# Macaron block on one core: routing steps and the attention's transposes placed one unit of experts later

## Chip, cores and metric

One core of one Trainium2 chip. The metric is the device time of one execution in microseconds, the median of the runs of a kernel. The kernel before ran three times: 587.32, 587.5 and 589.16 us, median 587.5.

## The reference

2048 tokens of width 128 pass three steps: half of a mixture-of-experts layer, an attention, half of the same mixture-of-experts layer again, each on a layer norm of its input and added to it.

```python
x = x + 0.5 * ffn(layernorm(x))
x = x + attn(layernorm(x))          # softmax over all 2048 tokens
x = x + 0.5 * ffn(layernorm(x))
# ffn: shared = silu(x @ Ws_up) @ Ws_down                     (64 hidden)
#      aff = x @ centroids.T ; the 8 of 64 experts with the largest aff + bias
#      w = sigmoid(aff) of those 8, divided by their sum, 0 for the other 56
#      result = shared + sum over experts of w_e * (silu(x @ W_up[e]) @ W_down[e])
```

## The kernel before

**Tiling.** The tokens are cut into 4 chunks of 512. The two mixture-of-experts layers make 8 chunks, n = 0 to 7 (chunk c of layer f is n = 4f + c); the attention lies between n = 3 and n = 4. All 64 experts are computed for all tokens, two experts at a time, so that hidden values fill 128 partitions. A chunk has 33 units: unit 0 is the shared expert (64 partitions), units 1 to 32 are pairs of experts. Each product of float32 quality is three matmuls of rounded parts (high times low, low times high, high times high).

**One unit u.** TensorE makes the hidden values in one of 4 PSUM buffers (`up`, L805 to L807). ScalarE applies silu in place (L380). VectorE multiplies by the experts' weights, spread over partitions in `wide` (`gate_unit`, L552). ScalarE copies the result as the high part (`hi_unit`, L391). The low part, the difference (`low_part`, L240), is made by GpSimd (POOL) in units where u % 3 is 1 or 2, and by VectorE in units where u % 3 is 0. TensorE multiplies by the down weights (`down`, L843 to L845) and accumulates over the 33 units. `down` runs 4 units behind `up`: in unit u TensorE does up(u), then down(u-4). up(u) reuses the hidden buffer of unit u-4, so it waits for gate(u-4) where GpSimd makes that unit's low part, and for the low part itself where VectorE does.

**Order of the work.** Each engine has its own loop over the units, written out by hand; `if u == ...` puts extra steps after the unit's own instructions. An engine does its instructions in this order and waits on semaphores at each. Within VectorE's unit u stand gate(u), then lo(u-1) if VectorE makes it, then the extra steps. ScalarE's unit has silu(u), hi(u-1), extra steps. GpSimd's unit has lo(u), if it is GpSimd's, and then its extra steps.

**Extra steps for the next chunk n+1** (`pro_...`, in chunks that have a next one in their layer: n = 0, 1, 2, 4, 5, 6): the layer norm's statistics (VectorE, u 0 and 2), rstd (GpSimd, u 3), normed values xn (VectorE, u 5 and 6, lines L575 to L579), their transposes `pro_xT` (TensorE, u 8, L856), split into high and low part (ScalarE u 9, VectorE u 9), affinities `pro_aff` (TensorE u 11, 12 matmuls; read by VectorE at u 12 and 13, L596 to L600), a reciprocal (`pro_top` 0, L607, u 14), top 8 (u 15, L611), and the mask of the chosen (u 17, L616, L618). `weights` (GpSimd, u 18, L332 and L333) waits for the mask; `pro_sum` (VectorE, u 20, L635 to L637) waits for `weights`; `normed_weights` (GpSimd, u 21, L338) waits for `pro_sum`; `pro_cw` (TensorE, u 24, L876) transposes; `pro_cwT` (ScalarE, u 25, L407) copies to `gates`. SyncE's queue (SP) stores them to DRAM and then loads them back, spread over 64 partitions each, one pair of loads a unit, up to 6 units ahead (`wide`, L299); its wait for `gates` stands before the loads of unit STORE = 30.

**Extra steps for the chunk before** (`epi_...`): the output is scaled (ScalarE u 5), transposed `epi_yT` (TensorE u 8, L849), added to x (VectorE u 9). In the first layer (n = 1, 2, 3) the attention's inputs follow: statistics (VectorE u 10), rstd (GpSimd u 14), normed xn2 (VectorE u 16 and 17), transposes `epi_xT` (TensorE u 20, L856), split `epi_hi` (ScalarE u 21) and `epi_lo` (VectorE u 21, L646), projections `epi_proj` (TensorE u 24, 28, 31).

**Counting.** `on_pool` decides who makes the low part; it makes some positions differ from their neighbours:

```python
def on_pool(u):
    return u % 3 != 0
```

Of the kernel before, what the change touches and what calls it, by code (L numbers as in the profile page):

```python
# [30 lines left out]
NH = 4  # L31
NB = 6
EARLY = 4
STORE = 30
GT = 2
PRE = 8
LEAD = 2
# [6 lines left out]
def macaron_kernel(nc, x_d, wup_d, wdn_d, wsup_d, wsdn_d, cent_d, bias_d, wq_d, wk_d, wv_d, gates_d, out_d):  # L44
# [21 lines left out]
    with ExitStack() as ctx:  # L66
# [146 lines left out]
        def on_pool(u):  # L213

            return u % 3 != 0
# [91 lines left out]
        @block.gpsimd  # L307
        def _(pool):
            steps = [0]

            def link(ins):

                steps[0] += 1
                ins.then_inc(s_pool, 1)
                pool.wait_ge(s_pool, steps[0])

            def rstd(k, n, stats, done):

                pool.wait_ge(stats, n + 1)
                ve, y = (rs[:, k, i, :] for i in range(2))  # L320
                link(nc.gpsimd.tensor_scalar(ve, mv[:, k, :, 1], EPS, None, ALU.add))
                nc.gpsimd.tensor_tensor(y, ve, mhalf[:, :], ALU.pow).then_inc(done, 1)

            def piece_lo(k):
                pool.wait_ge(s_whi, k + 1)
                nc.gpsimd.tensor_tensor(piece(k, 1), raw[:, k % NR, :], piece(k, 0).bitcast(F32), ALU.subtract).then_inc(s_w, 1)

            def weights(n):

                pool.wait_ge(p_sil, n + 1)  # L330
                pool.wait_ge(p_top, n + 1)
                link(nc.gpsimd.tensor_tensor(rec[:, :, :], rec[:, :, :], sil[:, :, :], ALU.mult))  # L332
                nc.gpsimd.tensor_tensor(rec[:, :, :], rec[:, :, :], rest[:, :, :], ALU.mult).then_inc(p_w, 1)  # L333

            def normed_weights(n):
                pool.wait_ge(p_inv, n + 1)
                inv = wsum[:, 1, :].unsqueeze(2).to_broadcast([P, TPC, E])
                nc.gpsimd.tensor_tensor(cw2[:, :, 0:E], rec[:, :, :], inv, ALU.mult).then_inc(p_cw, 1)  # L338

            link(nc.gpsimd.memset(ident[:, :], 0.0))  # L340
            nc.gpsimd.affine_select(out=ident[:, :], in_=ident[:, :], compare_op=ALU.not_equal, fill=1.0,
                                    base=0, pattern=[[-1, P]], channel_multiplier=1).then_inc(s_id, 1)
            link(nc.gpsimd.memset(mhalf[:, :], -0.5))
            for f in range(2):
                for c in range(NCH):
                    n = f * NCH + c
                    if c == 0:
                        rstd(0, n, p_st, p_rs)
                    if n == 0:
                        for k in range(PRE):  # L350
                            piece_lo(k)
                    for u in range(UNITS):
                        if on_pool(u):
                            low_part(nc.gpsimd, n * UNITS + u).then_inc(s_glop, 1)
                        if n == 0 and u % 2 == 0 and PRE + u // 2 < 2 * WP:
                            piece_lo(PRE + u // 2)
                        if c + 1 < NCH:
                            if u == 3:
                                rstd(0, n + 1, p_st, p_rs)
                            if u == 18:  # L360
                                weights(n + 1)
                            if u == 21:
                                normed_weights(n + 1)
                        if f == 0 and c and u == 14:
                            rstd(1, c - 1, e_st, e_rs)
                if f == 0:
                    rstd(1, NCH - 1, e_st, e_rs)

        @block.scalar
        def _(act):  # L370
# [66 lines left out]
            for f in range(2):  # L437
                for c in range(NCH):
                    n = f * NCH + c
                    if c == 0:  # L440
                        if f == 0:
                            piece_hi(0)
                            pro_hi(n)
                            for k in range(1, 6):
                                piece_hi(k)
                            pro_sil(n)
                            for k in range(6, PRE):
                                piece_hi(k)
                            for u in range(LEAD):
                                silu_unit(u, n)  # L450
                            pro_cwT(n)
                    for u in range(UNITS):
                        if c or u >= LEAD:
                            silu_unit(u, n)
                        if n == 0 and u % 2 == 0 and PRE + u // 2 < 2 * WP:
                            piece_hi(PRE + u // 2)
                        if u or c:
                            hi_unit(*((u - 1, n) if u else (UNITS - 1, n - 1)))
                        if c + 1 < NCH:
                            if u == 9:  # L460
                                pro_hi(n + 1)
                            if u == 15:
                                pro_sil(n + 1)
                            if u == 25:
                                pro_cwT(n + 1)
                        if c:
                            if u == 5:
                                epi_y(n - 1)
                            if f == 0 and u == 21:
                                epi_hi(c - 1)  # L470
                            if f == 0 and u in (25, 29, 32)[:1 if c == NCH - 1 else 3]:
                                epi_proj_hi(c - 1, (25, 29, 32).index(u))
                    if c == NCH - 1:
                        hi_unit(UNITS - 1, n)
                        if f == 0:
                            epi_proj_hi(c - 1, 1)
                        epi_y(n)
                        if f == 0:
                            epi_proj_hi(c - 1, 2)
                            epi_hi(c)  # L480
                            epi_proj_hi(c, 0)
                            epi_proj_hi(c, 1)
# [46 lines left out]
        def _(dve):  # L529
# [140 lines left out]
            for f in range(2):  # L670
                for c in range(NCH):
# [15 lines left out]
                    for u in range(UNITS):  # L687
# [3 lines left out]
                        if c + 1 < NCH:  # L691
                            if u == 0:
                                if f == 0:
                                    dve.wait_ge(s_x[c + 1], 16)
                                raw_stats(0, c + 1, (0, 1))
                            if u == 2:
                                stats(0, c + 1, p_st, (2, 3))
                            if u == 5:
                                normed(0, n + 1, c + 1, xn[f], p_rs, p_xn, (0, 1))
                            if u == 6:  # L700
                                normed(0, n + 1, c + 1, xn[f], p_rs, p_xn, (2, 3))
                            if u == 9:
                                pro_lo(n + 1)
                            if u == 12:
                                pro_aff(n + 1, 0)
                            if u == 13:
                                pro_aff(n + 1, 1)
                            if u == 14:
                                pro_top(n + 1, 0)
                            if u == 15:  # L710
                                pro_top(n + 1, 1)
                            if u == 17:
                                pro_top(n + 1, 2)
                            if u == 20:
                                pro_sum(n + 1)
                        if c:
                            if u == 9:
                                epi_x(n - 1, c - 1)
                            if f == 0:
# [3 lines left out]
                                    normed(1, c - 1, c - 1, xn2, e_rs, e_xn, (0, 1))  # L723
                                if u == 17:
                                    normed(1, c - 1, c - 1, xn2, e_rs, e_xn, (2, 3))
                                if u == 21:
                                    epi_lo(c - 1)
                                if u in (25, 29, 32)[:1 if c == NCH - 1 else 3]:
                                    epi_proj_lo(c - 1, (25, 29, 32).index(u))
# [72 lines left out]
        def _(pe):  # L802
# [107 lines left out]
            for f in range(2):  # L910
                for c in range(NCH):
# [10 lines left out]
                    for u in range(UNITS):  # L922
# [5 lines left out]
                        elif c:  # L928
                            down(UNITS - LAG + u, n - 1)
                        if c + 1 < NCH:  # L930
                            if u == 8:
                                pro_xT(n + 1)
                            if u == 11:
                                pro_aff(n + 1)
                            if u == 24:
                                pro_cw(n + 1)
                        if c:
                            if u == 8:
                                epi_yT(n - 1)
                            if f == 0:  # L940
                                if u == 20:
                                    epi_xT(c - 1)
                                if u in (24, 28, 31)[:1 if c == NCH - 1 else 3]:
                                    epi_proj(c - 1, (24, 28, 31).index(u))
# [117 lines left out]
```

## Time and profile before

| | us |
|---|---|
| median of 3 runs | 587.5 |
| the profiled execution, device time | 589.12 |
| its span, first to last instruction | 587.3 |
| TensorE matmul busy | 547.0 (93%) |
| VectorE busy | 440.8 (75%) |
| ScalarE busy | 408.0 (69%) |
| GpSimd busy | 274.8 (47%) |
| mean granted TensorE clock | 0.983 of full |

The profiled execution took 589.12 us on the device, 1.8 more than its span; that is 1.6 above the median, near the slowest of the three. Chunks begin at 14.20, 78.20, 134.72 and 190.17 us in the first layer, and at 381.72, 431.09, 481.25 and 531.39 in the second. Busy times of TensorE overlap, since matmuls are pipelined: it is better read by the starts of its instructions. "L805" is line 805 of the kernel. In a timeline, "x2" after a row means that two instructions in a row are merged, and the bracket tells how long the engine stood idle before and what released it.

### The profile page before, as it was taken

The numbers are of one execution on the slowest core, as the hardware profiler recorded it, in microseconds if no ns is written. First come the engines' busy times: TensorE is split into PE (matmuls) and PEld (weight loads), VectorE is DVE, ScalarE is ACT, GpSimd is POOL, SyncE is SP. The second block draws the span as 40 slices with busy tenths as digits, with TensorE's granted clock in tenths as the row PEclk, the third lists the DMA queues.
The fourth block names the chain that finished last, engine by engine and source line by source line (L and its number), as shares of the span: only waits on it lengthen the run. The fifth ranks groups of instructions, "written<-read, shape, count | busy, mean of one in ns | idle before, by whom it ended". The sixth has DMA issues, their size and how long they took to land.

```text
span 587.3 us, 8657 instructions
## 1 busy us (share of the span) xinstructions
PE 547.0 (93%) x2720; PEld 446.0 (76%) x2720; DVE 440.8 (75%) x913; ACT 408.0 (69%) x802; POOL 274.8 (47%) x241
## 2 busy tenths in 40 slices
PE   2489999899989999889999999899999999999996
PEld 2368777687768787668999989868777787877884
DVE  3787869967996587557677888888868958875663
ACT  3567776677767778356666665677776787687774
POOL 4478764656465666400000000045765666566563
PEclk9999999899999999969999999999999999999999
DMA  5465564355445555000000000036554465656552
GB/s 166 151 198 183 172 194 147 135 168 166 146 133 183 164 159 179 1 1 1 2 0 2 1 2 1 1 117 196 174 192 150 156 207 146 176 167 200 182 188 84
DMA packets 47837, 73.25 MB, mean 125 GB/s; under 512 B 8944, under 2 KB 13488, under 8 KB 47792
## 3 DMA queue, kind: packets, MB, share of 16 engines
q1 hardware_dynamic: 47792, 72.71, 39.5%
q8 instruction: 21, 0.34, 0.2%
q14 instruction: 24, 0.20, 0.1%
HBM read 70.58 MB, written 2.10 MB: 124 GB/s over the span
## 4 chain that ended last, share of the span: by engine, by line
PE 76%; DVE 13%; issue 3%; ACT 3%; DMA 2%; POOL 2%; SPq 1%; POOLq 0%; DVEq 0%; ACTq 0%
PE lrow L805 12%; PE lrow L807 11%; PE lrow L806 11%; PE bank L843 8%; PE bank L844 8%; PE bank L845 8%; PE bank L849 6%; PE bank L986 3%; PE bank L988 3%; PE bank L987 3%; DVE gated L552 2%; DVE rs L577 2%; DVE rs L575 1%; PE bank L807 1%; PE bank L806 1%
## 5 line engine op out<-in xcount | busy, mean ns | idle before, releaser
L240 POOL TENSOR_TENSOR gpart_lo<-gated,gpart_hi 128x512 fp32r<-128x512 f32 x176 | 226.6, 1294 | 197.8 <-ACT gpart_hi L391 194.2
L380 ACT ACTIVATE lrow<-lrow 128x512 f32<-128x512 f32 (+1 forms) x256 | 149.7, 585 | 63.5 <-PE lrow L807 62.0
L552 DVE TENSOR_TENSOR gated<-lrow,wide 128x512 f32<-128x512 f32 x170 | 116.5, 685 | 50.2 <-ACT lrow L380 46.4
L391 ACT CAST gpart_hi<-gated 128x512 fp32r<-128x512 f32 x176 | 107.9, 613 | 8.3 <-DVE gated L552 7.7
L843 PE MATMUL bank<-gpart_lo,wdn_hi 128*128 128x512 f32 x256 | 102.2, 399 | 1.1 <-POOL gpart_lo L240 1.0
L844 PE MATMUL bank<-gpart_hi,wdn_lo 128*128 128x512 f32 x256 | 101.3, 396 | 0.0
L845 PE MATMUL bank<-gpart_hi,wdn_hi 128*128 128x512 f32 x256 | 101.1, 395 | 0.0
L552 DVE TENSOR_TENSOR lrow<-lrow,wide 128x512 f32<-128x512 f32 x78 | 54.0, 693 | 28.7 <-ACT lrow L380 28.7
L391 ACT CAST gpart_hi<-lrow 128x512 fp32r<-128x512 f32 (+1 forms) x88 | 52.0, 591 | 30.4 <-DVE lrow L552 30.2
L751 DVE TENSOR_TENSOR pT_lo<-bank,pT_hi 128x512 fp32r<-128x512 f32 x64 | 43.7, 684 | 24.5 <-ACT pT_hi L496 23.7
L240 DVE TENSOR_TENSOR gpart_lo<-lrow,gpart_hi 128x512 fp32r<-128x512 f32 (+1 forms) x88 | 59.9, 681 | 1.3 <-ACT gpart_hi L391 0.6
L843 PEld LDWEIGHTS bank<-gpart_lo,wdn_hi 128*128 128x128 f32 x256 | 48.4, 189 | 14.0 <-POOL gpart_lo L240 3.1
L845 PEld LDWEIGHTS bank<-gpart_hi,wdn_hi 128*128 128x128 f32 x256 | 48.5, 190 | 11.4
L844 PEld LDWEIGHTS bank<-gpart_hi,wdn_lo 128*128 128x128 f32 x256 | 48.5, 190 | 10.9
L489 ACT ACTIVATE prow<-lrow,nmax 128x512 f32<-128x512 f32 x64 | 44.3, 694 | 14.8 <-DVE nmax L664 14.8
L496 ACT CAST pT_hi<-bank 128x512 fp32r<-128x512 f32 x64 | 37.9, 592 | 23.8 <-PE bank L849 23.6
L805 PE MATMUL lrow<-xnT_lo_a,wup_hi 128*128 128x512 f32 x128 | 53.5, 418 | 0.5 <-DVE gpart_lo L240 0.5
L805 PE MATMUL lrow<-xnT_lo_b,wup_hi 128*128 128x512 f32 x128 | 52.5, 410 | 0.0
L807 PE MATMUL lrow<-xnT_hi_a,wup_hi 128*128 128x512 f32 x128 | 51.7, 404 | 0.0
L806 PE MATMUL lrow<-xnT_hi_a,wup_lo 128*128 128x512 f32 x128 | 51.7, 404 | 0.0
L807 PE MATMUL lrow<-xnT_hi_b,wup_hi 128*128 128x512 f32 x128 | 50.5, 395 | 0.0
L806 PE MATMUL lrow<-xnT_hi_b,wup_lo 128*128 128x512 f32 x128 | 50.1, 391 | 0.0
(171 smaller groups left out, 997.6 us busy)
## 6 DMA issues: line engine op xcount, KB each, us to landing
wide<-gates_dram SPq DMA_DIRECT2D x496, 128.0 KB, 3.0
raw<-in_w_up SPq DMA_DIRECT2D x8, 256.0 KB, 3.6
raw<-in_w_down SPq DMA_DIRECT2D x8, 256.0 KB, 3.9
x<-in_x SPq DMA_DIRECT2D x4, 256.0 KB, 4.0
gates_dram<-gates SPq DMA_DIRECT2D x8, 128.0 KB, 2.2
out_dram<-x SPq DMA_DIRECT2D x4, 256.0 KB, 3.2
raws<-in_wq SPq DMA_DIRECT2D x1, 64.0 KB, 2.1
raws<-in_wk SPq DMA_DIRECT2D x1, 64.0 KB, 2.1
```

What stands on the lines that cost most here:

```text
L240: return eng.tensor_tensor(gpart[1][0:m, U % NGP, :], gated_at(U)[0:m, :], gpart[0][0:m, U % NGP, :].bitcast(F32), ALU.subtract)
L380: nc.scalar.activation(dst[0:m, :], hid[U % NH][0:m, :], ACT.Silu).then_inc(s_silu, 1)
L391: nc.scalar.copy(gpart[0][0:m, U % NGP, :], gated_at(U)[0:m, :]).then_inc(s_ghi, 1)
L489: nc.scalar.activation(prow[:, j * CH:(j + 1) * CH], lrow[:, j * CH:(j + 1) * CH], ACT.Exp, bias=nmax[:, t % 2:t % 2 + 1], accum_out=psums ...
L552: nc.vector.tensor_tensor(gated_at(U), a, b, ALU.mult).then_inc(s_gated, 1)
L751: nc.vector.tensor_tensor(pT[1][at], tb[q % 2][:, :].rearrange("p (k n) -> p k n", n=P), pT[0][at].bitcast(F32), ALU.subtract).then_inc(a_ ...
L805: nc.tensor.matmul(out, a[0], b[1], start=True, stop=False)
L806: nc.tensor.matmul(out, a[1], b[0], start=False, stop=False)
L807: return nc.tensor.matmul(out, a[0], b[0], start=False, stop=True)
L843: nc.tensor.matmul(y, w[0], g[1], start=(u == 0), stop=False)
L844: nc.tensor.matmul(y, w[1], g[0], start=False, stop=False)
L845: nc.tensor.matmul(y, w[0], g[0], start=False, stop=(u == UNITS - 1)).then_inc(s_down, 1)
```

## The change

Steps are placed one unit later on every engine: on GpSimd `weights` (18 to 19) and `normed_weights` (21 to 22); on ScalarE `pro_hi`, `pro_sil`, `pro_cwT` and `epi_hi`; on VectorE `pro_lo`, both steps of `pro_aff`, the three of `pro_top`, `pro_sum` and `epi_lo`; on TensorE `pro_xT`, `pro_aff`, `pro_cw` and `epi_xT`; on SyncE's queue the store of the gates (30 to 31). The norms (VectorE u 5, 6, 16, 17), `epi_yT`, `epi_x`, rstd and the projections stay.

```diff
-STORE = 30
+STORE = 31
 # GpSimd
-                            if u == 18:
+                            if u == 19:
                                 weights(n + 1)
-                            if u == 21:
+                            if u == 22:
                                 normed_weights(n + 1)
 # ScalarE
-                            if u == 9:
+                            if u == 10:
                                 pro_hi(n + 1)
-                            if u == 15:
+                            if u == 16:
                                 pro_sil(n + 1)
-                            if u == 25:
+                            if u == 26:
                                 pro_cwT(n + 1)
-                            if f == 0 and u == 21:
+                            if f == 0 and u == 22:
                                 epi_hi(c - 1)
 # VectorE
-                            if u == 9:
+                            if u == 10:
                                 pro_lo(n + 1)
-                            if u == 12:
+                            if u == 13:
                                 pro_aff(n + 1, 0)
-                            if u == 13:
+                            if u == 14:
                                 pro_aff(n + 1, 1)
-                            if u == 14:
+                            if u == 15:
                                 pro_top(n + 1, 0)
-                            if u == 15:
+                            if u == 16:
                                 pro_top(n + 1, 1)
-                            if u == 17:
+                            if u == 18:
                                 pro_top(n + 1, 2)
-                            if u == 20:
+                            if u == 21:
                                 pro_sum(n + 1)
-                                if u == 21:
+                                if u == 22:
                                     epi_lo(c - 1)
 # TensorE
-                            if u == 8:
+                            if u == 9:
                                 pro_xT(n + 1)
-                            if u == 11:
+                            if u == 12:
                                 pro_aff(n + 1)
-                            if u == 24:
+                            if u == 25:
                                 pro_cw(n + 1)
-                                if u == 20:
+                                if u == 21:
                                     epi_xT(c - 1)
```

## Rows read from the trace of the kernel before

**Rows 1.** The page: the chain that ended last, by engine.
```profile
PE 76%; DVE 13%; issue 3%; ACT 3%; DMA 2%; POOL 2%; SPq 1%; POOLq 0%; DVEq 0%; ACTq 0%
```
**Rows 2.** Timeline of TensorE, chunk 5, pro_xT and up(10): start us, us, instruction, [idle].
```profile
444.92 0.59 PE L856 MATMUL bank<-ident,xn_b 128*128 128x128 f32 x2 [0.49 <-DVE xn_b L579]
...
447.17 0.40 PE L805 MATMUL lrow<-xnT_lo_b,wup_hi 128*128 128x512 f32 x1
```
**Rows 3.** Timeline of VectorE: xn (2,3) and lo(6) of chunk 5; lo(6) of chunk 4.
```profile
444.53 0.59 DVE L579 TENSOR_SCALAR xn_b<-x,mv,rs 128x128 f32<-128x128 f32 x2
...
445.64 0.68 DVE L240 TENSOR_TENSOR gpart_lo<-lrow,gpart_hi 128x512 fp32r<-128x512 f32 x1
...
395.91 0.68 DVE L240 TENSOR_TENSOR gpart_lo<-lrow,gpart_hi 128x512 fp32r<-128x512 f32 x1
```
**Rows 4.** Timeline of TensorE: chunk 4's up(10); chunk 1's epi_xT (unit 20), up(26).
```profile
397.01 0.40 PE L805 MATMUL lrow<-xnT_lo_b,wup_hi 128*128 128x512 f32 x1
...
112.61 0.33 PE L856 MATMUL bank<-ident,xn 128*128 128x128 f32 x1 [1.57 <-DVE xn L579]
...
123.06 0.39 PE L805 MATMUL lrow<-xnT_lo_a,wup_hi 128*128 128x512 f32 x1
```
**Rows 5.** Windows after that wait, chunks 1 and 2: us, busy, PEclk, DMA share, GB/s.
```profile
113.38:116.80 3.42, 3.42 (x10) 2.65 (x11) 3.32 (x6) 2.91 (x6) 1.83 (x2) 0.53 0.27 93
...
169.90:173.26 3.36, 3.14 (x13) 2.27 (x14) 3.26 (x6) 2.86 (x6) 1.77 (x2) 1.00 0.26 93
```
**Rows 6.** Timeline of VectorE, chunk 5: gate(12), aff, gates 13, 16, mask, 19, lo(18), sum, 22.
```profile
452.81 0.70 DVE L552 TENSOR_TENSOR lrow<-lrow,wide 128x512 f32<-128x512 f32 x1 [1.44 <-ACT lrow L380]
453.42 0.41 DVE L596 TENSOR_SCALAR rec<-bank 128x256 f32<-128x256 f32 x1
...
454.21 0.69 DVE L552 TENSOR_TENSOR gated<-lrow,wide 128x512 f32<-128x512 f32 x1
...
459.10 0.67 DVE L552 TENSOR_TENSOR gated<-lrow,wide 128x512 f32<-128x512 f32 x1
...
461.77 1.55 DVE L618 TENSOR_TENSOR rest<-rest,biased_b 128x256 f32<-128x256 f32 x1
...
463.85 0.67 DVE L552 TENSOR_TENSOR gated<-lrow,wide 128x512 f32<-128x512 f32 x1
464.59 0.69 DVE L240 TENSOR_TENSOR gpart_lo<-lrow,gpart_hi 128x512 fp32r<-128x512 f32 x1
...
466.24 0.73 DVE L636 TENSOR_SCALAR wsum<-wsum 128x4 f32<-128x4 f32 x1
...
467.69 0.68 DVE L552 TENSOR_TENSOR gated<-lrow,wide 128x512 f32<-128x512 f32 x1
```
**Rows 7.** Timeline of GpSimd, chunk 5: lo(16) and lo(17), weights, lo(19) and lo(20), normed weights.
```profile
460.50 2.54 POOL L240 TENSOR_TENSOR gpart_lo<-gated,gpart_hi 128x512 fp32r<-128x512 f32 x2 [1.63 <-ACT gpart_hi L391]
463.47 0.75 POOL L332 TENSOR_TENSOR rec<-rec,sil 128x256 f32<-128x256 f32 x1 [0.42 <-DVE rest L618]
464.30 0.74 POOL L333 TENSOR_TENSOR rec<-rec,rest 128x256 f32<-128x256 f32 x1
465.65 2.54 POOL L240 TENSOR_TENSOR gpart_lo<-gated,gpart_hi 128x512 fp32r<-128x512 f32 x2 [0.61 <-ACT gpart_hi L391]
468.15 0.61 POOL L338 TENSOR_TENSOR cw<-rec,wsum 128x256 f32<-128x256 f32 x1
```
**Rows 8.** Instructions of line L618, minimum, median and maximum in ns.
```profile
L618 DVE TENSOR_TENSOR rest<-rest,biased_b x4: 425/1556/1557, 376.1 to 511.9; 128x256 f32<-128x256 f32 x4
```
**Rows 9.** Timeline of TensorE, chunk 5: up(22) and up(26).
```profile
465.34 0.50 PE L805 MATMUL lrow<-xnT_lo_b,wup_hi 128*128 128x512 f32 x1
...
471.47 0.40 PE L805 MATMUL lrow<-xnT_lo_b,wup_hi 128*128 128x512 f32 x1
```
**Rows 10.** Timeline of TensorE, chunk 3: down(17) in unit 21.
```profile
221.29 0.50 PE L843 MATMUL bank<-gpart_lo,wdn_hi 128*128 128x512 f32 x1
```
**Rows 11.** Timeline of SyncE's queue, chunk 5: the store of the gates.
```profile
472.55 0.48 SPq L280 DMA_DIRECT2D gates_dram<-gates  x1
```

## The prediction

> **What bounds the kernel now.** First the chain that ended last: TensorE holds 76% of it, VectorE 13% and GpSimd 2% [rows 1]. So TensorE's stream of matmuls sets the time, and the other engines count only where TensorE waits for them. Next, therefore, the starts of `up` in TensorE's timeline, unit by unit. From up(22) to up(26) of chunk 5 pass 6.13 us [rows 9]; less some 0.55 for `pro_cw` and two restarts, that is 1.40 us a unit, six matmuls at full rate. A unit that takes longer has an extra step or a wait. The waits that stand out are two. In each of the six chunks with a next one, `pro_xT` waits in unit 8 for the last normed tiles: 0.49 us on the matmul row, 0.8 in the stream with the restart [rows 2, 3]. And in chunks 1 and 2 `epi_xT` waits in unit 20 for xn2, 1.57 us and a bit more [rows 4]. After that wait the granted clock was 0.53 for 3.4 us in chunk 1 (near the lower of the two levels, 1.2 GHz) and 1.00 in chunk 2 after the same wait [rows 5]: the penalty is not regular.
>
> Then VectorE's timeline between units 12 and 24, which shows how little slack lies behind TensorE. In chunk 5 gate(12) comes after 1.44 us idle, and from there the engine works without a pause until lo(18) at 464.59, and up(22), which needs lo(18), starts at 465.34, 0.75 later, at once [rows 6, 9]. GpSimd has room there: after lo(17) it stands idle and takes `weights` (0.83 + 0.74 = 1.57 us) ahead of lo(19) [rows 7].
>
> **What is moved, and what it saves.** Nothing is added or removed; every instruction stays on its engine, so only waits can change.
>
> *`pro_xT`, unit 8 to 9.* Its last tile xn starts at 444.53 [rows 3], and TensorE now comes to it a unit (1.40) later, so this wait goes. What is late next is lo(6), which frees the buffer of up(10): it starts at 445.64 [rows 3], +0.75 gives 446.39, against up(10) at 447.17 before [rows 2]. Saved: 0.78. Chunk 6 repeats chunk 5, and chunks 1 and 2 show the same pattern. In chunk 4 lo(6) at 395.91 gives 396.66 against 397.01 [rows 3, 4]: 0.35 saved. In chunk 0, where unit 8's wait is longer but lo(6) is as late, I take 0.35 too.
>
> *`pro_hi`, `pro_lo`, `pro_aff` on TensorE* move together with it, in units where nobody waited: 0. Their cover is VectorE's idle 1.44 before gate(12) [rows 6]; TensorE's 12 short matmuls now stand ahead of up(13), and that idle time moves to before gate(13).
>
> *The first half of the routing, on VectorE.* Before, the first affinity step (0.79, from 453.42 to 454.21) ran between gate(12) and gate(13) [rows 6]. Now it follows gate(13). In chunk 5, with the 0.78 gained, gate(13) comes at 453.43. From gate(13) to the mask L618 it was 7.56; to that come 0.79 and one gate, 0.60, since gate(18) is now ahead of it: L618 at 462.4. Such a gate is followed on GpSimd by its low part 1.40 later (459.10 to 460.50), which takes 1.27 [rows 6, 7]; so lo(17) runs from 461.7 to 462.9.
>
> What L618 costs there: it took 0.43 us at its shortest and 1.56 at its median [rows 8]; in chunk 5 it ended at 463.32, just behind GpSimd's lo(17) (460.50 + 2.54 = 463.04) [rows 6, 7]. So I read its length as a wait for that operation and let it end at 463.2, 0.3 after lo(17), and not 1.55 after its start. The Trainium skill, page "SBUF — State Buffer", section "SBUF: two separate sides", states that VectorE and GpSimd share a port pair as an exclusive lock, held for the whole instruction by whichever starts first; by that L618 ends with lo(17), as I take it, while with a fixed 1.55 up(22) would wait 0.7 longer, and the sum below would be about 4 us more. The trace agrees with the lock (0.43 alone against 1.56).
>
> Then gate(19) 463.15, lo(18) 463.75, up(22) at 464.5, where TensorE wants it (465.34 - 0.78 = 464.56). No wait, the gain is still there.
>
> *The second half: `weights`, `pro_sum`, `normed_weights`.* Here the positions matter. Units 18 and 21 are multiples of 3, in which GpSimd has no low part; 19 and 22 are not. `weights` now stands behind lo(19), and `normed_weights` behind lo(22). Chunk 5: lo(19) 464.55 to 465.82; `weights` to 467.39 (+1.57). VectorE, through with gate(21) at about 465.6, stands in `pro_sum` waiting for it, with gate(22) and lo(21) queued behind: 1.8 us. GpSimd then runs lo(20) until 468.66; TensorE wants it for down(20) at 464.56 + 2 x 1.40 + 0.70 = 468.05 and waits 0.6. The second step of `pro_sum`, 0.73 long before and then ending with lo(19) (466.97 against 466.92) [rows 6, 7], now ends with lo(20), at 468.7. gate(22) 468.8 (467.69 before), lo(21) 469.4, so up(25) at 470.15, where TensorE would have been at 469.4 even after the first wait: 0.7 more. lo(22) 470.2 to 471.47, `normed_weights` (0.61) to 472.1; TensorE reaches `pro_cw` at 470.15 + 1.40 = 471.55 and waits 0.55. With the transposes (0.36) and restart, up(26) is at 472.55 against 471.47 [rows 9]. **Net in chunk 5: +1.1 us**, although 0.8 had been gained.
>
> *Copies and stores behind it.* `pro_cwT` then ends near 475 and the store goes out some 2.5 us after 472.55 [rows 11]. What queues behind it on SP are the loads for units 31 and 32 and of the next chunk, 6 units (8 us) ahead of use: 0, as the landing takes 3 us. Were that cover gone, each late load would cost its lateness once.
>
> *`epi_xT`, unit 20 to 21, `epi_hi`, `epi_lo` (chunks 1 and 2).* The mask now stands behind the norms, so xn2 is ready near 110.3 and the transposes' wait of 1.57 goes. But gate(17) stands behind the norm's first half at 109.2, lo(17) runs to 111.85, and down(17), wanted at 110.6, waits 1.3; lo(18) makes up(22) wait 0.4 (113.4); then as above `weights` ends at 116.3, lo(20) at 117.55 (wait 0.65), and `epi_lo`, last in VectorE's unit 22 (118.9), releases the first projection at 119.6 (wait 1.3). Then there is no wait at `pro_cw`, and up(26) is at 122.2 against 123.06 [rows 4]: -0.9. Chunk 2, 1.1 us shorter before because the clock stayed up, ends the same: +0.2. Chunk 3 has no next chunk; there down(17) waited for lo(17) until 221.29 [rows 10], after the transposes, which had run within that wait; now they come after it: +0.35.
>
> **The sum.** Chunk 0 +1.5, 1 -0.9, 2 +0.2, 3 +0.35, 4 +1.5 (chunk 5's 1.1 + 0.78 - 0.35), 5 and 6 +1.1 each, 7 and attention 0: **+4.85 us**. Against the profiled execution: span 587.3 to 592.1, device time 589.12 to 594.0. Its own time is 1.6 above the median 587.5, so the median should go to 592.3 us. Bounds for what no row shows, the phase between VectorE and GpSimd in the new order: at best the second-half chain costs half (0.9 a chunk instead of 1.85 in chunks 0, 4, 5, 6, 0.5 less in 1 and 2), sum about 0; at worst VectorE's tiny steps each meet a GpSimd operation and lose up to 0.7 more a chunk, sum near 9.
>
> **The rivals.** A measurement of this kernel tells 0.3%, 1.8 us, from no change.
>
> *A, the forecast*: up to half the gains kept, the GpSimd chain costs more. Chance 0.59, 589.5 to 595.5.
>
> *B, the same with the clock falling.* Three waits within 4 us come where two did. A stretch at 0.53 for 3.42 us [rows 5] loses 1.6 us. For it: chunk 1. Against: chunk 2, same wait, no fall. In three chunks it would be +4.8, some 597. Chance 0.14.
>
> *C, faster.* The waits at xn and xn2 go and nothing takes their place: 4 x 0.78 + 2 x 0.35, and what unit 20's wait cost with the slow stretch, 4.0 in chunk 1 and 3.0 in chunk 2; 10.8 in all, 576.7 us. It is decided at `pro_sum`: if `weights` is done when VectorE gets there (I have it 1.8 us late), nothing queues. For it: VectorE's queue may be later than I have it, so that it covers the wait. Against: the four units of lead are TensorE's only slack and rows 6 and 9 show it used up. Chance 0.14; most of it lies at 580 to 585.
>
> *D, no difference.* Gains and chain cancel, the bound at best above: 587.5. Chance 0.13.
>
> Faster by over 0.3% 0.14, within 0.3% 0.13, slower 0.73. The range 587 to 597 leaves out C and the tail of B.
>
> **What would show it.** Right: units 8 lose their wait; VectorE stands idle ahead of `pro_sum`'s reduce (L635) for over 1 us, released by GpSimd's L333; TensorE waits in units 24 and 25, for low parts of GpSimd and VectorE and for `cw`; `epi_proj` waits for x2T_lo; `weights` comes after lo(19). Wrong: L635 without idle time before it, or up(26) no later than before in chunks 5 and 6; or a wait of the loads (`wide`), which I put at 0.

## The result, and the profile after

The changed kernel took 593.59 us (median of 4 runs, 593.07 to 594.83) against 587.6 (4 runs, 587.32 to 589.16): ratio 1.0092, 95% interval 1.0073 to 1.0112. It is slower by 0.9% (the two medians alone give 1.0102, inside the interval); the forecast was 592.3 in a range of 587 to 597. The profiled execution took 593.69 us, its span 591.9.

The page of the changed kernel, the lines that answer to the table of before and to [rows 1]:

```profile
span 591.9 us, 8657 instructions
PE 546.1 (92%) x2720; PEld 440.9 (74%) x2720; DVE 434.8 (73%) x913; ACT 408.8 (69%) x802; POOL 274.2 (46%) x241
PE 65%; DVE 15%; POOL 8%; issue 4%; ACT 4%; DMA 2%; SPq 1%; POOLq 0%; DVEq 0%; ACTq 0%
```

The same instructions, the same count; VectorE is even 6 us less busy, 4.5 of them in the mask L618, which waits less (8 times, 10.0 us in all before and 5.5 after). But the chain that ended last has 8% on GpSimd where it had 2%, and 65% on TensorE where it had 76%. Its waits say where, with the total in us, the number of times and the longest:

```profile
PEld bank L843 <- POOL gpart_lo L240: 11.7, 13, 1.5
DVE wsum L635 <- POOL rec L333: 10.2, 6, 1.7
PEld lrow L805 <- DVE gpart_lo L240: 6.8, 13, 1.1
PEld bank L876 <- POOL cw L338: 3.0, 4, 0.8
```

Before, the first line read 3.1 us in 5 times, the third 2.4 in 5, and the second had no entry at all.

GpSimd in chunk 5, which starts at 433.20 here and at 431.09 before; compare [rows 7]:

```profile
463.89 1.29 POOL L240 TENSOR_TENSOR gpart_lo<-gated,gpart_hi 128x512 fp32r<-128x512 f32 x1 [0.40 <-ACT gpart_hi L391]
466.80 1.30 POOL L240 TENSOR_TENSOR gpart_lo<-gated,gpart_hi 128x512 fp32r<-128x512 f32 x1 [1.62 <-ACT gpart_hi L391]
468.06 0.73 POOL L332 TENSOR_TENSOR rec<-rec,sil 128x256 f32<-128x256 f32 x1
468.87 0.73 POOL L333 TENSOR_TENSOR rec<-rec,rest 128x256 f32<-128x256 f32 x1
469.56 1.28 POOL L240 TENSOR_TENSOR gpart_lo<-gated,gpart_hi 128x512 fp32r<-128x512 f32 x1
472.43 1.30 POOL L240 TENSOR_TENSOR gpart_lo<-gated,gpart_hi 128x512 fp32r<-128x512 f32 x1 [1.59 <-ACT gpart_hi L391]
473.68 0.62 POOL L338 TENSOR_TENSOR cw<-rec,wsum 128x256 f32<-128x256 f32 x1
```

The order is lo(17), lo(19), `weights`, lo(20), lo(22), `normed_weights`. The engine stands idle 1.62 us before lo(19) although the mask has been ready since 465.5, and does `weights` only afterwards.

VectorE in the same stretch (compare [rows 6]), from the mask on:

```profile
464.57 0.90 DVE L618 TENSOR_TENSOR rest<-rest,biased_b 128x256 f32<-128x256 f32 x1
465.39 0.68 DVE L552 TENSOR_TENSOR gated<-lrow,wide 128x512 f32<-128x512 f32 x1
465.99 0.67 DVE L240 TENSOR_TENSOR gpart_lo<-lrow,gpart_hi 128x512 fp32r<-128x512 f32 x1
...
469.64 0.42 DVE L635 TENSOR_REDUCE wsum<-rec 128x4 f32<-128x256 f32 x1 [1.70 <-POOL rec L333]
470.09 0.78 DVE L636 TENSOR_SCALAR wsum<-wsum 128x4 f32<-128x4 f32 x1
...
471.01 0.69 DVE L552 TENSOR_TENSOR gated<-lrow,wide 128x512 f32<-128x512 f32 x1
471.62 0.68 DVE L240 TENSOR_TENSOR gpart_lo<-lrow,gpart_hi 128x512 fp32r<-128x512 f32 x1
```

L635 comes after 1.70 us of waiting for L333, with gate(22) (471.01) and lo(21) (471.62) behind it. And TensorE (compare [rows 2, 9]):

```profile
448.51 0.50 PE L805 MATMUL lrow<-xnT_lo_b,wup_hi 128*128 128x512 f32 x1
...
466.72 0.50 PE L805 MATMUL lrow<-xnT_lo_b,wup_hi 128*128 128x512 f32 x1
...
470.90 0.50 PE L843 MATMUL bank<-gpart_lo,wdn_hi 128*128 128x512 f32 x1 [0.42 <-POOL gpart_lo L240]
...
472.35 0.50 PE L805 MATMUL lrow<-xnT_lo_b,wup_hi 128*128 128x512 f32 x1 [0.50 <-DVE gpart_lo L240]
...
474.35 0.63 PE L876 MATMUL bank<-ident,cw 128*64 128x128 f32 x4 [0.34 <-POOL cw L338]
474.74 0.47 PE L805 MATMUL lrow<-xnT_lo_b,wup_hi 128*128 128x512 f32 x1
```

Counted from the chunk's start, up(10) is at 15.31 us (16.08 before: 0.77 gained), up(22) at 33.52 (34.25 before: still gained), and then come three waits, at down(20), up(25) and `pro_cw`. up(26) is at 41.54 against 40.38: 1.16 lost.

The same reading for each chunk, in us against the trace of before (chunk 5's and 6's lengths: 51.40 and 51.36 against 50.15; chunk 3 is read at its last `up`; the attention is the stretch from there to the first `up` of chunk 4):

| | chunk 0 | 1 | 2 | 3 | attention | 4 | 5 | 6 | sum |
|---|---|---|---|---|---|---|---|---|---|
| forecast | +1.5 | -0.9 | +0.2 | +0.35 | 0 | +1.5 | +1.1 | +1.1 | +4.85 |
| measured | +1.52 | -0.61 | +0.47 | +0.46 | -1.31 | +1.64 | +1.24 | +1.22 | +4.63 |

Not all of these figures repeat from trace to trace, which the experiments below need. In a second trace of the kernel before, chunk 0 was 0.50 shorter and chunk 1 was 1.05 shorter (its slow stretch of [rows 5] was absent); chunks 2 to 6 were as long to 0.04. So every figure for chunk 1 that is taken against the first trace, here and below, makes the other version look 1.05 better than it is, where its own trace has no such stretch: against the second trace the changed kernel's chunk 1 stands at +0.44, like chunk 2. The attention, too, has one length in some traces and another in others (last experiment).

### The profile page after: what moved, and what is told of

It is laid out like the page before. It is cut to its first block, busy times and chain, and to the rows that moved or that the text cites. A ratio compares the mean times of both kernels' runs of the same rounds, so it can differ in the third digit from the quotient of the medians.

```text
span 591.9 us, 8657 instructions
## 1 busy us (share of the span) xinstructions
PE 546.1 (92%) x2720; PEld 440.9 (74%) x2720; DVE 434.8 (73%) x913; ACT 408.8 (69%) x802; POOL 274.2 (46%) x241
## 4 chain that ended last, share of the span: by engine, by line
PE 65%; DVE 15%; POOL 8%; issue 4%; ACT 4%; DMA 2%; SPq 1%; POOLq 0%; DVEq 0%; ACTq 0%
PE lrow L805 10%; PE lrow L807 9%; PE lrow L806 9%; PE bank L843 7%; PE bank L845 6%; PE bank L844 6%; PE bank L849 5%; POOL gpart_lo L240 5%; DVE gated L552 3%; PE bank L986 3%; PE bank L988 3%; PE bank L987 3%; DVE gpart_lo L240 2%; ACT gpart_hi L391 2%; DVE rec L607 1%
```

## The experiments

Ratios are to the kernel before on the same chip; there its median was 589.3 to 589.4 us, so that ratios, not times, are to be compared over the groups.

**GpSimd's two steps put back in the changed kernel.**

```diff
-                            if u == 19:
+                            if u == 18:
                                 weights(n + 1)
-                            if u == 22:
+                            if u == 21:
                                 normed_weights(n + 1)
```

> The changed kernel with GpSimd's two steps alone put back: weights in unit 18, normed_weights in unit 21; everything else stays one unit later. Theory (the loss comes from weights standing behind lo(19), so that pro_sum on VectorE waits 1.7 us for it, and from normed_weights standing behind lo(22)): the idle time of VectorE before L635 falls from 10.2 us to under 1, TensorE's waits in units 24 and 25 of chunks 0, 4, 5, 6 vanish, while the gain of the later pro_xT stays. up(26) against the kernel before: -0.3 in chunks 0 and 4, -0.75 in 5 and 6, -2.4 and -1.4 in 1 and 2, +0.5 in 3: about 582 us, faster than both kernels. Rival (VectorE's own later order, lo(21) and epi_lo behind more work, makes TensorE late): the waits in units 24 and 25 stay, 592 us or more.

Measured: 581.29 us, ratio 0.9865 (0.984 to 0.9891). Two places of an `if` turn a loss of 0.9% into a gain of 1.35%. GpSimd and VectorE in chunk 5, where lo(17) is at 454.97:

```profile
454.97 1.30 POOL L240 TENSOR_TENSOR gpart_lo<-gated,gpart_hi 128x512 fp32r<-128x512 f32 x1 [0.39 <-ACT gpart_hi L391]
456.69 0.74 POOL L332 TENSOR_TENSOR rec<-rec,sil 128x256 f32<-128x256 f32 x1 [0.42 <-DVE rest L618]
457.51 0.74 POOL L333 TENSOR_TENSOR rec<-rec,rest 128x256 f32<-128x256 f32 x1
458.20 2.56 POOL L240 TENSOR_TENSOR gpart_lo<-gated,gpart_hi 128x512 fp32r<-128x512 f32 x2
...
458.93 0.41 DVE L635 TENSOR_REDUCE wsum<-rec 128x4 f32<-128x256 f32 x1
```

`weights` runs in what was GpSimd's idle time before lo(19), and L635 has no wait, in any of the six chunks. Read at up(28), behind all extra steps of the next chunk, the chunks stand against the trace of before at -1.32, -2.72, -1.64, +0.44, -0.43, -0.76 and -0.77 (0 to 6): 5 and 6 as expected, 4 better by 0.1, 1 and 2 by 0.3 and 0.2. The gain as a whole is larger than expected: some 8 us against the 589.34 of this chip, where about 582 against 587.5 had been 5.5. In the trace, 1.0 of the difference is chunk 0 and 1.2 the attention, neither of which repeats. Chunk 0's figure differs by 1.5 us between two versions whose order of steps in it is the same (+1.52 in the changed kernel, +0.05 with the attention's steps put back), so it can carry no argument.

**The same two steps moved alone, in the kernel before** (18 to 19, 21 to 22).

> The kernel before with GpSimd's two steps alone moved: weights to unit 19, normed_weights to unit 22. Theory: pro_sum, here still in VectorE's unit 20, stands some 2.7 us waiting for weights behind lo(19), and normed_weights comes behind lo(22), which needs gate(22), which is behind pro_sum; pro_cw, still in TensorE's unit 24, waits about 4 us for it. Some 4 us in each of six chunks: about 612 us, far slower than the change as a whole. Rival (where GpSimd's two steps stand does not matter, since GpSimd is idle half of the time): 587.5 us.

Measured: 625.14 us, ratio 1.061 (1.0594 to 1.0625): +36 us, the theory's sign and mechanism, and nearly half as much again as it said. The waits of that kernel:

```profile
PEld bank L876 <- POOL cw L338: 23.6, 6, 4.1
DVE wsum L635 <- POOL rec L333: 15.7, 6, 2.6
```

2.6 us at L635 and 4 at `pro_cw`, as reckoned. What was missing is for the most part the clock: chunks 1 and 2 lost 4.9 and 6.0, the others 6.0 to 7.4. After such a wait the granted clock falls, as these windows of its chunk 4 show (the stretch with the wait, the 4.8 us from `pro_cw` on, and the next 9 us; us, busy time of PE, PEld, DVE, ACT and POOL, then PEclk, DMA share and GB/s):

```profile
436.00:441.24 5.24, 1.16 (x4) 0.49 (x4) 4.15 (x8) 2.62 (x5) 2.69 (x4) 1.00 0.33 93
441.24:446.00 4.76, 4.76 (x16) 3.87 (x17) 1.29 (x2) 2.12 (x5) 1.19 (x1) 0.64 0.33 96
446.00:455.00 9.00, 9.00 (x40) 7.10 (x39) 5.83 (x9) 7.11 (x14) 5.18 (x4) 1.00 0.67 196
```

0.64 for 4.76 us is 1.7 us of work at full speed. What a chunk loses by it is less: chunk 5, where the granted clock was 0.50 for 6.8 us, is 1.3 us longer than chunk 6, where it was so for half as long. By this estimate the clock costs 1.3 of the 6.0 us in chunks 2, 4 and 6, and the waits 4.7, somewhat more than the 4 expected.

**One of the two put back at a time, in the changed kernel.** `weights` alone, 19 to 18:

> The changed kernel with weights alone put back to unit 18; normed_weights stays in unit 22. Theory: pro_sum no longer waits, which is most of the loss; pro_cw waits at most 0.2 us behind lo(22) and normed_weights: about 583 us. Rival (normed_weights behind lo(22) is the costlier half): about 590 us.

Measured: 581.11 us, ratio 0.9865 (0.9844 to 0.9886), not to be told from both put back. `normed_weights` alone, 22 to 21:

> The changed kernel with normed_weights alone put back to unit 21; weights stays in unit 19. Theory: pro_sum still waits 1.7 us in each of six chunks; only the wait at pro_cw goes (0.65 us with its restart in chunks 0, 4, 5, 6): about 591 us. Rival (as above, normed_weights is the costlier half): about 585 us.

Measured: 591.53 us, ratio 1.0065 (1.0032 to 1.0098); L635 still waits 10.2 us in 6 times. Its nine runs spread from 589.89 to 597.64 us, the widest of all versions, and why was not found; their median alone would give 1.0037, just inside the interval. Chunks 5 and 6 stand at +0.68 and +0.69 instead of +1.24 and +1.22. So `weights` behind lo(19) is the cause; with it back, `normed_weights` in unit 22 costs nothing that these runs can tell, and TensorE has no wait at `pro_cw`.

**The first half alone, in the kernel before** (`pro_xT`, `pro_hi`, `pro_lo`, `pro_aff`, `pro_sil`, `pro_top` one unit later, the rest as it was).

> The kernel before with the first half alone moved one unit later: pro_xT, pro_hi, pro_lo, pro_aff, pro_sil and the three steps of pro_top; weights, pro_sum, normed_weights, pro_cw, pro_cwT, the store and the attention's steps stay. Theory: all of the gain and none of the chain on GpSimd; up(26) against the kernel before -0.75 in chunks 5 and 6, -0.3 to -0.4 in 4, some 2 us in 1 and 2, 0 in 3; ratio to the kernel before 0.986, as with GpSimd's steps put back. Rival (the second half needs the same distance to the first, so that pro_sum waits for weights again as the mask is a unit later): L635 idle over 1 us, ratio 1.00 or more.

Measured: 580.58 us, ratio 0.9856 (0.9835 to 0.9878). Chunks 1 to 6: -2.64, -1.67, 0.00, -0.43, -0.72, -0.71. The whole gain lies in the first half; the second half's move gained nothing, and cost where it took GpSimd's steps along. L635 did not wait.

**The attention's steps put back in the changed kernel** (`epi_xT` 21 to 20, `epi_hi` and `epi_lo` 22 to 21).

> The changed kernel with the attention's steps put back (epi_xT in unit 20, epi_hi and epi_lo in 21). Theory: of the gain in chunks 1 and 2 little hangs on these, since xn2 is early because the mask now stands behind the norms and up(22) is held by lo(18); chunk 3 gets its 0.46 back, chunks 1 and 2 gain 0.2 each at the projection: 1 us less than the changed kernel, ratio to the kernel before 1.007. Rival (moving epi_xT is what removed the wait in unit 20): chunks 1 and 2 lose over 1.5 us each, ratio 1.014.

Measured: 593.1 us, ratio 1.007 (1.0052 to 1.0088). Chunk 3 back to +0.01, chunks 1 and 2 at -0.80 and +0.27 instead of -0.61 and +0.46. The move of `epi_xT` itself gained nothing.

**Both GpSimd's and the attention's steps put back.**

> The changed kernel with both GpSimd's steps and the attention's steps put back; a candidate for the best order. Theory: as with GpSimd's steps alone put back (ratio 0.9865), less the 0.46 us of chunk 3: ratio 0.986. Rival (epi_xT back in unit 20 waits for xn2 again): over 1.5 us each in chunks 1 and 2, ratio 0.992.

Measured: 581.21 us, ratio 0.9875 (0.9848 to 0.9903). Chunk 3 is back at 0.00 and chunks 1 and 2 keep their gain (-2.73, -1.66), as expected; the 0.46 us of chunk 3 is too little to be told from the ratio 0.9865 of the version before it.

**The mask alone, in the kernel before.**

```diff
-                            if u == 17:
+                            if u == 18:
                                 pro_top(n + 1, 2)
```

> The kernel before with one step moved: the mask (pro_top 2) from VectorE's unit 17 to 18, behind the norms and gate(18). Theory: it is this step, and not epi_xT's own place, that ends the wait for xn2 in unit 20; up(22) is then held by lo(18) alone: chunks 1 and 2 shorter by 1.6 to 2.7 each, chunks 4, 5, 6 unchanged, ratio to the kernel before 0.993. Rival (TensorE has to come later for xn2): the wait in unit 20 stays over 1 us, ratio 1.00.

Measured: 583.43 us, ratio 0.991 (0.9893 to 0.9926). Chunks 1 and 2: -2.68 and -1.62, all that these chunks gain in any version; TensorE's weight loads wait for the layer-normed xn of L579 7.4 us in 5 times before and 2.7 in one here, the one between chunk 3 and the attention. That up(22) is held by lo(18) alone is not quite so: in chunk 1 its weight load waits 1.0 us for lo(18), and another 0.6 for a low part of GpSimd. One step of the nineteen that the change moves carries over half of the gain.

**The first half with the mask left in unit 17.**

> The kernel before with pro_xT, pro_hi, pro_lo, pro_aff, pro_sil and the first two steps of pro_top one unit later, the mask left in unit 17. Theory: pro_xT's wait goes, up(10) starts 0.75 us earlier as in the changed kernel, but the mask then stands ahead of gate(18) with the affinity step behind gate(13), lo(18) comes no earlier than before and up(22) gives the gain back: chunks 4, 5, 6 within 0.2 us of the kernel before, the wait for xn2 in chunks 1 and 2 as before; ratio 1.00. Rival (the gain at pro_xT stands by itself): -0.75 us in chunks 1, 2, 5 and 6, -0.3 in 0 and 4, ratio 0.994.

Measured: 589.1 us, ratio 0.9998 (0.9986 to 1.0011). TensorE in its chunk 5 has, from 440 to 475 us, one wait over 0.15 us. The gain at `pro_xT` is there (up(10) 0.76 us earlier), and up(22) gives it back waiting for lo(18), 1.05 us on the row of its weight load: chunks 5 and 6 end at +0.03 and +0.04. Chunk 4 ends at +0.42, more than the 0.2 that I allowed: it gives back the same 0.8 us between up(10) and up(22) as the others, where only 0.36 had been gained. Chunk 0, of which nothing was expected, ends at +0.94.

Why the mask's place decides this is in the rows of VectorE and GpSimd. With the whole first half moved (ratio 0.9856, above), chunk 5 starting at 424.60:

```profile
455.30 1.29 POOL L240 TENSOR_TENSOR gpart_lo<-gated,gpart_hi 128x512 fp32r<-128x512 f32 x1 [0.40 <-ACT gpart_hi L391]
455.98 0.90 DVE L618 TENSOR_TENSOR rest<-rest,biased_b 128x256 f32<-128x256 f32 x1
457.40 0.68 DVE L240 TENSOR_TENSOR gpart_lo<-lrow,gpart_hi 128x512 fp32r<-128x512 f32 x1
```

With the mask left in unit 17, chunk 5 starting at 432.19:

```profile
462.88 1.29 POOL L240 TENSOR_TENSOR gpart_lo<-gated,gpart_hi 128x512 fp32r<-128x512 f32 x1 [0.40 <-ACT gpart_hi L391]
462.96 1.49 DVE L618 TENSOR_TENSOR rest<-rest,biased_b 128x256 f32<-128x256 f32 x1
465.72 0.69 DVE L240 TENSOR_TENSOR gpart_lo<-lrow,gpart_hi 128x512 fp32r<-128x512 f32 x1
466.46 0.19 PEld L805 LDWEIGHTS lrow<-xnT_lo_b,wup_hi 128*128 128x128 f32 x1 [1.05 <-DVE gpart_lo L240]
```

VectorE has the same instructions ahead of lo(18) in both. But left in unit 17 the mask L618 starts 0.08 us after GpSimd's lo(17) and lasts 1.49 us; behind gate(18) it starts 0.68 after it and lasts 0.90. Both end 0.28 to 0.29 us after lo(17) does. lo(18) starts 32.80 us into the chunk in the one and 33.53 in the other: 0.59 of these 0.73 us is the mask held up by GpSimd for longer. The rest comes at lo(18) itself, which waits a little for ScalarE's high part.

So the effects don't add: `pro_xT`'s move alone is worth nothing and the mask's move 0.15 us in chunks 5 and 6, both together 0.72.

**The kernel before once more, for its trace.**

> The kernel before once more, for its trace alone. In the attention, which the change does not touch, the changed kernel's trace is 1.3 us shorter than the trace of before, whose mean clock from 245 to 290 us was 0.89 against 0.92. Theory: that is chance of the clock, and this second trace gives an attention of another length, 1 us or more off. Rival: the attention really is shorter behind the changed kernel, and this trace repeats that of before within 0.2 us.

Measured: attention 145.16 us against 145.21. By the letter of that expectation the rival came true. But over all twelve traces this stretch has one of two lengths, 143.9 to 144.1 (the changed kernel and four of the experiments) or 145.2 to 145.5 (the kernel before twice, and five others), and versions that differ in nothing near it fall in either: the changed kernel 143.9, with the attention's steps back 145.4, with those and GpSimd's back 145.5, with GpSimd's alone 144.0. The granted clock tells the two apart: over this stretch it is 0.98 in all five traces of the shorter length and 0.96 in all seven of the longer, as here in the kernel before and in the changed kernel (the columns as above; the clock is the third number from the end):

```profile
236.52:381.72 145.20, 137.38 (x922) 121.87 (x921) 108.24 (x240) 91.33 (x216) 5.70 (x7) 0.96 0.00 1
238.29:382.19 143.90, 135.48 (x922) 120.10 (x921) 108.25 (x240) 91.23 (x216) 5.69 (x7) 0.98 0.00 1
```

So the 1.3 us goes with the clock, as the theory had it, and not with the change; what makes the clock stay low for longer in one execution was not found. In the second trace of the kernel before chunk 1 was 55.47 us long instead of 56.52, chunk 2's length to 0.03: the slow stretch of [rows 5] was absent, and with it 1.05 us.

## Why the prediction was right

*What bounds the kernel.* Right: TensorE's stream, with VectorE's queue between units 12 and 24 just in time. The slack at up(22) was as tight as said: the first half without the mask shows it giving back all that unit 8 had gained.

*`pro_xT` and lo(6).* 0.78 was forecast for chunks 1, 2, 5, 6; the changed kernel's up(10) is 0.80, 0.79, 0.76 and 0.78 earlier. In chunk 4 0.35, measured 0.36. As forecast, lo(6) is late next.

*First half on VectorE, L618.* Right. The mask ends just behind lo(17): 465.47 against 463.89 + 1.29 = 465.18, and takes 0.90 us instead of 1.55. In chunk 1, where it began as lo(17) ended (113.36 against 112.17 + 1.27 = 113.44), it took 0.43. Taken at a fixed 1.55, the sum would have been about 9. The lock that the Trainium skill states on its page "SBUF — State Buffer" (section "SBUF: two separate sides") agrees with these three lengths, and with the 1.49 us above: in chunks 0, 4, 5 and 6 of the trace of before and of the changed kernel the mask starts while a low part of GpSimd runs, and ends 0.28 to 0.29 us after it whatever its own length.

*Second half.* Every link is in the rows: 1.70 us at L635 (forecast 1.8), gate(22) 1.21 later than before counted from the chunk's start (1.1), up(26) +1.16 (1.1). From up(22) to up(26) the chunks lose 1.88 in 4, 5 and 6, where the forecast had 1.85. The three waits on TensorE were forecast at 0.6, 0.7 and 0.55; with the time that a restart takes they are 0.6 (470.90 against 470.31), 0.65 (472.35 against 471.70) and 0.5 (474.35 against 473.86).

*`epi_xT`.* Right in its sum, the terms each a little off: -0.61 and +0.47 against -0.9 and +0.2. In chunk 1 the four waits in TensorE's stream (down(17), up(22), down(20), first projection) are 1.2, 0.4, 0.6 and 1.2 us against 1.3, 0.4, 0.65 and 1.3, so the missing 0.3 is not in them; it builds up in small pieces between: down(17) starts 0.1 later than reckoned, up(22) and the projection 0.2, up(28) 0.25 (the chunk's own later start, 1.46, taken off). The waits stand where it was said:

```profile
113.49 0.50 PE L843 MATMUL bank<-gpart_lo,wdn_hi 128*128 128x512 f32 x1 [1.03 <-POOL gpart_lo L240]
119.22 0.51 PE L843 MATMUL bank<-gpart_lo,wdn_hi 128*128 128x512 f32 x1 [0.47 <-POOL gpart_lo L240]
121.27 0.50 PE L805 MATMUL bank<-x2T_lo,small_hi 128*128 128x512 f32 x1 [1.09 <-DVE x2T_lo L646]
```

*The attention, put at 0,* was 1.31 shorter in the trace, by the clock, which made the span's sum (4.63) look closer to the forecast (4.85) than the units' own sum (5.94) was. The medians moved by 6.0.

*What was luck.* Chunk 0's +1.52 against a forecast of +1.5. Its up(10) was 1.03 us earlier where 0.35 was forecast, its up(8), ahead of every moved step, already 1.25 earlier, and the version with the attention's steps put back, which does the same in this chunk, came out at +0.05. Only the loss from up(22) to up(26), 1.95, is as in the other chunks. And -0.9 for chunk 1 was a forecast against a trace whose slow stretch does not repeat. That chunk 2 would gain less "because the clock stayed up" was rightly read: the second trace of before shows it.

*Copies and stores:* 0, right: the store went out at 477.3 in chunk 5, and no new wait for `wide` came up.

Rival B did not happen: idle times of 0.42, 0.50 and 0.34 us within 4 us did not lower the clock, which was 1.00 over chunks 4 to 6; in the kernel with GpSimd's steps moved alone one wait of 3.42 us did. B's price of 1.6 us for a slow stretch was too high: the two traces of before put it at 1.05. Rival C named the right point of decision, `pro_sum`: with `weights` in time the kernel goes to 0.9865, though not to the 576.7 us that C summed up, since in chunks 1 and 2 down(17) then waits for GpSimd's lo(17), 1.03 us on its row, and up(22) for lo(18), up to 0.4 us on the row of its weight load. Rival D is refuted by the interval.

**The best version found** is the kernel before with the first half alone one unit later: ratio 0.9856, 1.4% faster than before; with GpSimd's steps put back in the changed kernel it is 0.9865, and the two cannot be told apart.

## What to carry to other kernels

In a schedule written out by hand, "one unit later on every engine" is not a shift of the whole: a step lands in another phase of whatever alternates in the loop. Here GpSimd's free units were every third one, and a step moved out of its free unit queued behind work that waits for a later unit, while its consumer on VectorE waited with all that was behind it. Ask of each moved step which instruction now stands ahead of it on its engine and what that one waits for; an engine idle half of the time is no protection, for an in-order queue idles in front of ready work. And test moves in groups and apart: one of them gave nothing alone and 0.7 us a chunk with another, since what was late next, lo(18), had to come earlier too. It came earlier by no work taken away: the mask met GpSimd's instruction 0.6 us later in its course and was held up for so much less.

## What was not expected of the hardware

The same wait of 1.57 us before `epi_xT` cost 1.05 us more in one execution of the kernel before than in another (chunk 1, 56.52 against 55.47 us), by the granted clock of 0.53 for 3.4 us after it. And the attention comes in two lengths 1.3 us apart, each repeated within 0.4 us, over kernels that share every instruction of it; the granted clock over it is 0.98 in the one and 0.96 in the other.
